# Local-attention layers in one kernel: masks in row tiles, one rotation of all PSUM pairs, and a new order of stages

## The reference, cut to what matters

```python
for i in range(6):
    x = attn_layer(shift_tokens(x), Wqkv[i], q_scale[i], k_scale[i], Wo[i]) + x
    x = ffn_layer(shift_tokens(x), ln_g[i], ln_b[i], W1[i], b1[i], W2[i], b2[i]) + x

def attn_layer(x, Wqkv, qs, ksc, Wo):        # 16 heads of 64, windows of 32
    q, k, v = split(x @ Wqkv)                # 128 -> 3 * 1024
    q = l2norm(q) * qs;  k = l2norm(k) * ksc
    q = q * cos * scale + rotate_half(q) * sin * scale
    k = k * cos / scale + rotate_half(k) * sin / scale
    # each window of 32 queries sees its own and the previous window of keys
    sim = where(mask, -max, 8.0 * (q @ k.T))
    return (softmax(sim) @ v) @ Wo

def ffn_layer(x, g, b, W1, b1, W2, b2):      # 128 -> 2 * 341 -> 128
    a, gate = split((layernorm(x) * g + b) @ W1 + b1)
    return (a * gelu(gate)) @ W2 + b2
```

## Time and profile before

| | us |
|---|---|
| median of three runs | 3746.63 (3743.57 to 3747.31) |
| profiled execution | 3750.37 |
| its span, first to last instruction | 3748.6 |
| PE busy | 3555.1 |
| DVE busy | 2719.1 |
| ACT busy | 2447.7 |
| POOL busy | 2283.3 |

### The profile page before, as it was taken

One profiled execution on the slowest core, in us unless ns is written; L12 is line 12 of the kernel. 1 busy time (PEld: TensorE's weight loads), 2 busy tenths in 40 slices (PEclk: granted clock), 3 DMA queues, 4 the chain that ended last, 5 costly groups with the idle time before them and its releaser, 6 DMA issues.

```text
span 3748.6 us, 131464 instructions
## 1 busy us (share of the span) xinstructions
PE 3555.1 (95%) x57538; PEld 2099.7 (56%) x57538; DVE 2719.1 (73%) x3104; ACT 2447.7 (65%) x4388; POOL 2283.3 (61%) x1216
## 2 busy tenths in 40 slices
PE   8979999999999999999999999999999999997996
PEld 4535555555555555555555555555555555553554
DVE  6858777777777777777777777777777777763787
ACT  6856666666666666666666666666666666664985
POOL 1227666666666666666666666666666666652666
PEclk9989999999999999999999999999999999998998
DMA  2001111111111111111111111111112111120000
GB/s 86 2 1 42 36 36 32 46 47 42 36 31 36 53 40 38 36 36 47 45 40 36 35 32 53 42 41 36 30 37 58 32 40 36 36 58 2 2 10 15
DMA packets 90943, 134.71 MB, mean 36 GB/s; under 512 B 23686, under 2 KB 37380, under 8 KB 89988
## 3 DMA queue, kind: packets, MB, share of 16 engines
q1 hardware_dynamic: 90372, 126.29, 13.0%
HBM read 23.48 MB, written 2.10 MB: 7 GB/s over the span
## 4 chain that ended last, share of the span: by engine, by line
PE 81%; ACT 6%; DVE 6%; issue 5%; POOL 1%; DMA 0%; SPq 0%; POOLq 0%; DVEq 0%; ACTq 0%
PE psum L697 29%; PE psum L777 8%; PE psum L763 8%; PE psum L726 7%; PE psum L804 7%; PE psum L707 6%; PE psum L815 3%; PE psum L738 2%; PE psum L717 2%; DVE f_times_sin L1013 2%; ACT f_squares L874 2%; ACT f_probsT L906 1%; ACT x_expo L1446 1%; PE psum L786 1%; PE psum L794 1%
## 5 line engine op out<-in xcount | busy, mean ns | idle before, releaser
L1121 POOL TENSOR_TENSOR f_rotated<-f_times_cos,f_times_sin 128x1024 f32<-128x1024 f32 x384 | 906.4, 2361 | 527.3 <-DVE f_times_sin L1013 527.3
L697 PE MATMUL psum<-w_qkv,f_xs 128*128 128x512 f32 x2304 | 1135.7, 616 | 40.2 <-DVE f_times_sin L1013 35.4
L874 ACT ACTIVATE f_squares<-psum 128x1024 f32<-128x1024 f32 x384 | 393.8, 1026 | 530.1 <-PE psum L697 530.1
L1129 POOL TENSOR_TENSOR f_rotated<-f_rotated,f_rnorm 128x1024 f32<-128x1024 f32 x384 | 722.3, 1902 | 26.5 <-ACT f_rnorm L885 26.5
L1113 POOL TENSOR_TENSOR f_probs<-f_probs,f_rowsum 128x1024 f32<-128x1024 f32 x192 | 365.2, 1902 | 537.6 <-DVE f_rowsum L1051 537.6
L892 ACT COPY f_qkT<-psum 128x1024 f32<-128x1024 f32 x384 | 388.4, 1011 | 351.5 <-PE psum L707 346.6
L697 PEld LDWEIGHTS psum<-w_qkv,f_xs 128*128 128x128 f32 x2304 | 393.7, 191 | 362.0 <-issue 284.6
L1012 DVE TENSOR_TENSOR f_times_cos<-psum,rot 128x1024 f32<-128x1024 f32 x384 | 460.4, 1199 | 88.7 <-ACT f_squares L874 86.5
L1013 DVE TENSOR_TENSOR f_times_sin<-psum,rot 128x1024 f32<-128x1024 f32 x384 | 465.6, 1212 | 0.0
L1020 DVE TENSOR_REDUCE f_sumsq<-f_squares 128x16 f32<-128x1024 f32 x384 | 451.8, 1208 | 0.0
L707 PE MATMUL psum<-consts,f_rotated 128*128 128x128 f32 x3072 | 408.1, 278 | 44.8 <-DVE f_gelu L1075 27.7
(11 more groups left out here) (179 smaller groups left out, 5237.3 us busy)
## 6 DMA issues: line engine op xcount, KB each, us to landing
f_v_moved<-f_v SPq DMA_DIRECT2D x768, 128.0 KB, 2.5
w_qkv<-in_l_wqkv SPq DMA_DIRECT2D x18, 512.0 KB, 3.7
w_o<-in_l_wo SPq DMA_DIRECT2D x6, 512.0 KB, 4.4
w_qkv<-in_ctxT SPq DMA_DIRECT2D x1, 2048.0 KB, 8.3
out<-x_f_result SPq DMA_DIRECT2D x8, 256.0 KB, 2.2
w<-in_l_w SPq DMA_DIRECT2D x6, 341.0 KB
xres<-in_xT SPq DMA_DIRECT2D x1, 1536.0 KB, 8.8
x_ctx<-in_ctxT SPq DMA_DIRECT2D x1, 1536.0 KB, 12.0
```

The costliest lines, as they stand in the source:

```text
L697: mm = pe.matmul(pairs[i][:, j * BANK:(j + 1) * BANK], xs[g % 2][:, u % GB, :], w_qkv[:, part * INNER + j * BANK:part * INNER + (j + 1) * ...
L874: act.activation(squares[part][:, :], pairs[QK_PAIR], ACT.Square).then_inc(squared[part], 1)
L1121: pool.tensor_tensor(rotated[u % 2][:, part].rearrange("p h (s d) -> p s h d", s=2), halves(times_cos[part][:, :]), halves(times_sin[part] ...
L1129: pool.tensor_tensor(rt, rt, rnorm[u % 2][:, part * H:(part + 1) * H].unsqueeze(2).broadcast_to([P, H, HD]), ALU.mult).then_inc(normalised ...
```

## The change

Masks: the constants get 128 more columns. `mask_band` now holds the two kinds of mask rows (window 0 and all other windows, 32 rows each) once in rows 0 to 63 and again in rows 64 to 127, and the new `mask_pick` holds a 0/1 matrix that picks the row for each query. The mask product of bank 0 uses rows 0 to 63 and that of bank 1 rows 64 to 127, as tiles of 64 rows by 128 columns at two row positions.

Pairs: no stage has a pair of its own. Every fill takes the next of the four pairs in the order in which PE fills them (`ROTATING`).

Order: all engines have a new order of the stages within a step. On PE, q is followed by the mix, k, v, then (later) transposes and scores; transposed q comes before the scores and transposed k after them. The third tile of `mlp_up`, its gelu and hidden product, `mlp_down` and `add_down` have a lag of 11 in place of 10, `exponentials` 3 in place of 2, `mlp_root` and `mlp_affine` 9 in place of 8 and 10. The loops run one step longer.

```diff
-CONSTS = 2 * P + NEAR + 4 * HD + 4
+CONSTS = 3 * P + NEAR + 4 * HD + 4
...
+        mask_pick = sb("mask_pick", [P, P], BF16)
...
-            SCORE_PAIR, QK_PAIR = 0, 1
-            LAST = 11
-            ALTERNATING = (("mix", 4, 1), ("v", 2, 1), ("up0", 10, GB), ("mean", 6, GB), ("up1", 10, GB), ("variance", 7, GB),
-                           ("up2", 10, GB), ("probs", 3, 1), ("out", 4, GB), ("k", 1, 1), ("down", 10, GB), ("q", 1, 1))
+            LAST = 12
+            ROTATING = (("q", 0, 1), ("mix", 4, 1), ("k", 0, 1), ("up0", 10, GB), ("up2", 11, GB), ("v", 2, 1), ("up1", 10, GB),
+                        ("variance", 7, GB), ("qT", 1, 1), ("scores", 2, 1), ("down", 11, GB), ("probs", 3, 1), ("kT", 1, 1),
+                        ("mean", 6, GB), ("out", 4, GB))
...
-                        pair_of[stage, u // every] = 2 + turn % 2
+                        pair_of[stage, u // every] = turn % 4
...
-                    if part < 2:
-                        i, taken = QK_PAIR, (producted[part], u + 1)
-                    else:
-                        i, taken = pair_of["v", u], (v_copied, u + 1)
-                    banks.fill(pe, i, taken)
+                    i = pair_of["qkv"[part], u]
+                    banks.fill(pe, i, (producted[part] if part < 2 else v_copied, u + 1))
...
                 def scores(u):
-                    banks.fill(pe, SCORE_PAIR, (lowered, u + 1))
+                    i = pair_of["scores", u]
+                    banks.fill(pe, i, (lowered, u + 1))
...
                     for j in range(2):
-                        pe.matmul(pairs[SCORE_PAIR][:, j * BANK:(j + 1) * BANK], ident_bf[:, :],
-                                  mask_band[:, :, :].rearrange("p g n -> p (g n)"), start=True, stop=False)
+                        rows = slice(HD * j, HD * j + HD)
+                        pe.matmul(pairs[i][:, j * BANK:(j + 1) * BANK], mask_pick[rows, :],
+                                  mask_band[rows, :, :].rearrange("p g n -> p (g n)"), start=True, stop=False,
+                                  tile_position=(rows.start, 0))
...
                 for step in range(UNITS + LAST):
                     project(step, 0)
                     mix(step - 4)
+                    project(step, 1)
+                    mlp_up(step - 10, 0)
+                    mlp_up(step - 11, 2)
                     project(step - 2, 2)
-                    mlp_up(step - 10, 0)
-                    scores(step - 2)
-                    project(step, 1)
-                    mlp_mean(step - 6)
                     mlp_up(step - 10, 1)
                     mlp_variance(step - 7)
-                    mlp_up(step - 10, 2)
+                    transpose_qk(step - 1, 0)
+                    scores(step - 2)
+                    mlp_down(step - 11)
                     transpose_probs(step - 3)
+                    transpose_qk(step - 1, 1)
+                    mlp_mean(step - 6)
                     project_out(step - 4)
-                    transpose_qk(step - 1, 1)
-                    mlp_down(step - 10)
-                    transpose_qk(step - 1, 0)
...
                 for step in range(-1, UNITS + LAST):
+                    mlp_root(step - 9)
+                    exponentials(step - 3)
+                    reciprocal_norms(step - 1)
                     square(step, 0)
+                    copy_mix(step - 4)
+                    square(step, 1)
+                    mlp_gelu(step - 10, 0)
+                    mlp_shift(step - 5)
+                    mlp_gelu(step - 10, 1)
+                    mlp_affine(step - 9)
+                    mlp_square(step - 7)
+                    mlp_gelu(step - 11, 2)
+                    copy_v(step - 2)
+                    copy_qk(step - 1, 0)
                     prepare(step + 1)
-                    mlp_affine(step - 10)
-                    mlp_root(step - 8)
-                    mlp_square(step - 7)
-                    copy_mix(step - 4)
-                    reciprocal_norms(step - 1)
-                    mlp_shift(step - 5)
-                    mlp_gelu(step - 10, 0)
-                    copy_v(step - 2)
-                    square(step, 1)
                     mlp_log(step - 7)
-                    mlp_gelu(step - 10, 1)
-                    mlp_gelu(step - 10, 2)
                     copy_probs(step - 3)
                     copy_qk(step - 1, 1)
-                    exponentials(step - 2)
-                    copy_qk(step - 1, 0)
...
                     row_sums(step - 3)
                     products(step, 0)
+                    products(step, 1)
                     mlp_hidden(step - 10, 0)
-                    mlp_centre(step - 6)
+                    mlp_hidden(step - 11, 2)
+                    sum_squares(step, 0)
+                    mlp_hidden(step - 10, 1)
                     row_maxima(step - 2)
-                    mlp_hidden(step - 10, 1)
-                    mlp_hidden(step - 10, 2)
                     lower(step - 2)
-                    products(step, 1)
-                    add_out(step - 4)
-                    sum_squares(step, 0)
-                    add_down(step - 10)
                     sum_squares(step, 1)
                     clamp_norms(step)
+                    add_down(step - 11)
+                    mlp_centre(step - 6)
+                    add_out(step - 4)
...
                     mlp_scale(step - 9)
+                    normalise(step - 1, 0)
                     normalise_probs(step - 3)
                     normalise(step - 1, 1)
-                    normalise(step - 1, 0)
+                    rotate(step, 1)
                     rotate(step, 0)
-                    rotate(step, 1)
...
             dve.tensor_copy(ident_bf[:, :], ident).then_inc(masks_ready, 1)
+            dve.tensor_copy(mask_pick[:, :], consts[:, 2 * P + NEAR:3 * P + NEAR]).then_inc(masks_ready, 1)
...
+    kinds = np.concatenate([band[0:2 * WIN]] * 2)
+    row = np.arange(P)
+    kind = np.where(row < WIN, row, WIN + row % WIN)
+    pick = np.arange(P)[:, None] % (2 * WIN) == kind[None, :]
+    return np.concatenate([np.eye(P), kinds, past, pick] + both + [parts], axis=1).astype(np.float32)
```

45 lines of the change are left out of this document (23 added, 22 removed).

## The result

| | before, us | after, us |
|---|---|---|
| median of four runs each | 3746.97 | 3609.78 (3601.7 to 3612.55) |
| profiled execution | 3750.37 | 3601.70 |
| its span | 3748.6 | 3599.9 |

The ratio is 0.9629, with a 95% interval from 0.9609 to 0.9648: 137 us, 3.7% faster. 3596 was forecast, with a range from 3560 to 3675.

What follows compares the result with a forecast made beforehand. The prediction took PE's own queue, with 2.65 us of waits per group, as the bound. Masks 33, pairs and order 108 and start 9 sum to 150 us: 3600 from the profiled execution, 3596.5 on the median, range 3560 to 3675.

Steps and rivals of the forecast that it cites:

- The bound: PE's own queue bounds the kernel: 65.05 us per group of four steps, 2.65 us of it waits.
- Masks, 33 us: Mask products on PE as two overlapping row tiles: 0.17 us gained in each of 192 units, 33 us.
- Pairs and order, 108 us: Rotating all four pairs in the new order covers PE's waits: 2.25 us per group won, 48 groups, 108 us.
- Margins: Slack before PE wants a pair still being read; thinnest at v: 0.5 us in step 1, 0.3 in step 2.
- Table loads, nothing: ACT's four table loads a group in place of two, 1.28 us each, cost nothing by themselves.
- Rival C: A table load holds ACT for twice its bar, delaying v in step 2: 48 us, 3645; chance 0.03.
- Start, 9 us: At the start of the layers two of three 3.50 us waits between q and k projections go: 9 us gained.
- Tail, nothing, give or take 3: One step more at the end for the last MLP, with hardly any work: 0, give or take 3 us.
- A: Margins don't hold; ACT and DVE pass delays on at v or qT: 29 to 80 us, say 3645; chance 0.18.
- B: Masks gain nothing, from no row-tile overlap or a second shape change: 33 to 52 us less, 3640; chance 0.06.
- D: Waits lie in norms, square and products; spreading pairs moves them without shortening; only masks and start won: 3705; chance 0.06.
- E: Slower: with shared pairs a loop through scores, norms, square and products sets each step; 3764 at 16.4 us; chance 0.08.

Runs made afterwards that it cites:

- e5: The kernel before with only the mask change, fixed pairs and old order kept: 3732.85 us, ratio 0.9945.
- e7: The kernel after with one more 0.6 us copy on ACT ahead of every square of q: 3619.67 us, ratio 0.9644.
- e9: The kernel after with all three gelus in one step, ACT doing affine, square, copy of v, then third gelu: 3624.72 us, ratio 0.9656.
- e4: The kernel after with third up tile, gelu and hidden product in the step of the other two: 3653.34 us, ratio 0.974.
- e8: The kernel after with all three gelus in one step and the copy of v ahead of the third gelu on ACT: 3700.55 us, ratio 0.9857.
- after again: The unchanged kernel after, measured once more beside other versions on the same chip: 3609.54 us, ratio 0.9619.

## Why the prediction was right, and where not

**The bound.** PE's own queue, with 2.65 us of waits a group. Right: with the waits gone the time fell by 125.9 us between the first and the last output projection of the layers, and PE's products have no wait for another engine left in the steady groups.

**Masks, 33 us.** Too much by a third: 0.11 a unit, 21 us, by e5. It is the lower end of the range that the row-tile row gave. The overlap is there; the price of entering and leaving is what was mis-sized. The row gave 0.20 for it, and I counted with 0.14 to get 0.17. Half of 0.43 for the products leaves 0.10 in the masks' own 0.32, and the transposes ahead take 0.10 more: 0.20 again. The Trainium skill, TensorEngine Tiling (Array Packing), section Key Properties, says that a change of mode drains the engine. The trace agrees, and gives 0.1 us for it here.

**Pairs and order, 108 us.** 2.25 us a group forecast; 2.58 - 4 x 0.11 = 2.1 measured. The size is nearly right and its make-up is not, so there is luck in it. The waits went to the last one, 2.65, and v behind another projection or up costs 1.72 in place of 1.82 in all four steps, 0.42 a group, which the sum left out and the range had at half; 0.4 was kept in hand for the thin margins at v, and the margins held. What took it instead is in PE's own stream, and the prediction had none of it. Whoever stands behind the score products pays for leaving their tile mode: the transposes of the probabilities three times (0.93 for 0.87, 0.17 in all) and down (2.68 for 2.58, 0.10). To this come 0.09 at q behind the mean (1.91 for 1.82), 0.25 for the stretched score products and 0.07 for the mean, and 0.23 more in gaps in which PE waits for its instructions. 2.65 + 0.42 - 0.91 is 2.16, beside the 2.1 measured.

**Margins.** 0.5 and 0.3 us at v were 0.71 and 0.54. I had laid each handover out one after the other, at full bar length, where in the trace bars of ACT and DVE overlap the next one by up to 0.1: q's products end 6.17 and 6.44 us after q's start, where I had 6.3 and 6.6. e7 showed the margins in use: with 0.6 us more ahead of the square v starts no later, and only its second pass in step 2 is 0.07 late.

**Table loads, nothing.** Right, by e9. Rival C falls with it. The figure of the Trainium skill, ScalarE: Activation LUTs, section What ACT_TABLE_LOAD costs, 1.38 us of drain beside the 1.28 of the load, is in no row: the bar is 1283 ns and the next instruction follows in 0.02.

**What the order is for.** Not in the prediction: v's copy and the MLP's square are as near to their limits as the norms and products that I followed. I had followed the pairs of up0, up1 and up2 only, and did not ask what the pair of v does to the scores if the third gelu stays; e4 and e8 were 44 and 91 us slower by that.

**Start, 9 us.** From the first projection to the first output projection 98.7 became 88.4, 10.3 less; in the other execution of after it is 87.2. How much of it belongs to the shorter steps in that stretch was not separated. The first four projections run through without a wait, where one of 3.50 stood ahead of each but the first:

```profile
245.38 10.10 PE L699 MATMUL psum<-w_qkv,f_xs 128*128 128x512 f32 x16 [4.55 <-ACT f_xs L855]
```

**Tail, nothing, give or take 3.** Wrong in this pair of executions: from the last output projection but one to the end of the layers 85.7 us became 72.3. In its first half 45.1 became 40.3. The second half gave 8.7, of which 4.4 are clock and 4.3 are not. The windows over the last 42 us of the layers before, and the last 32 after (the column ahead of the last two is the clock):

```profile
3383.00:3425.00 42.00, 29.92 (x56) 11.60 (x56) 7.21 (x10) 13.17 (x17) 1.26 (x1) 0.87 0.00 1
```

```profile
3243.00:3275.00 32.00, 25.32 (x56) 9.68 (x56) 6.70 (x10) 12.89 (x17) 2.53 (x2) 1.00 0.00 1
```

At the lower clock the 16 passes of the last output projection took 8.6 us until DVE could read them (7.1 after), and the last up to add_down 12.8 (9.9 after): 4.4 together. Between them lie the MLP of the last group but one and the norm of the last, 16.3 us before (3395.24 to 3411.50) and 12.0 after (3252.94 to 3264.94), with PE's passes at full length in both. There the variance, which the last group's up waits for, stands behind down in the old order and ahead of it in the new one, and ACT's square behind three gelus and now behind two. The prediction had the tail at nothing without laying this chain out.

**Rivals.** A, B in part (0.06 of masks missing), C, D and E as whole cases did not come. D's thought, that pairs alone move waits without shortening, was right of the pairs alone, and stronger than thought.

## What to carry to other kernels

Once PE's waits on other engines are gone, count its queue by starts and look at which of its own groups grow: a change of tile mode is paid by its neighbour, and a transfer issued just ahead of many small products lengthened them whatever it moved. Where a long stream of small products has gaps that name no engine, compare them with the packets of the instruction queue. A rotation of buffers and the order of their readers are one thing: change either alone and a buffer comes round to a reader that stands late in an in-order queue. When an operation is moved across another on a reader's queue, list every pair that waits behind it, and not the one for which it was moved.

## What the hardware showed that I had not expected

Two things, beside the stretch of the score products (1.39 to 1.55 us) and the gaps in which PE waits for its instructions (0.27 us a group).

The granted clock differs between executions in the stretch ahead of the layers, which is the same code in after again and in the version with late transfers. Their first 100 us:

```profile
0.00:100.00 100.00, 80.33 (x880) 49.30 (x894) 73.81 (x89) 70.11 (x249) 15.42 (x27) 1.00 0.24 81
```

```profile
0.00:100.00 100.00, 84.00 (x783) 51.66 (x795) 66.52 (x81) 63.02 (x225) 14.96 (x26) 0.88 0.25 81
```

Clock 1.00 and 0.88, 880 and 783 products done in 100 us. The first output projection of the layers comes at 331.3 in the one and at 341.8 in the other. So in these two 10 us, against a scatter of 15 in the runs of after again (3601 to 3616), arise before the changed code is reached, and a comparison of spans can miss a gain of that size: the two profiled spans are 3599.3 and 3600.1, though a group takes 0.23 us less in the second. The end of the layers scatters too: from the last output projection to the last pass of down it is 31.4 us in after at a clock of 1.00 and 33.0 in after again at 0.95. The periods of these two executions, 62.37 both, don't have this noise.

And the granted clock was lower where PE waited much. From 600 to 3000 us PE is busy for 1976 of the 2400 us with the order of after and fixed pairs, at a clock of 0.95, and for 2158 with the pairs alone, at 0.97; before has 2350 and after 2392, both at 1.00. So a wait can cost more than its own length.
